# Scanning steps' orders made anew, and stage A's transposed x stored in DRAM and loaded by stage C in place of a second transpose

## What is computed

```
xr, gate = split(x @ W_in.T);  xr += cond
xc = silu(causal_conv4(xr) + b_conv)
xn = layernorm(xc) * g + b
B, C, dt = split(xn @ W_xproj.T);  dt = tanh(dt @ W_dt.T + b_dt) * 0.01
h_t = clip(h_{t-1} * (1 + dt_t * A) + B_t * min(|xn_t|, 1) * xn_t, -10, 10)   # 16 x 512 state per sequence
x1 = x + ((C_t . h_t) + D * xn) * silu(gate) @ W_out.T
z = layernorm(x1 * s1);  q, k, v = demodulated projections of z
out = x1 + demod(softmax(q k / 4) v @ W_w.T) + demod(v @ W_u.T)                # 16 heads of 16
```

## Time and profile before

| | us |
|---|---|
| median of 3 runs (1808.18 to 1811.61) | 1810.15 |
| the profiled execution, its own time | 1813.53 |
| its span, first to last instruction | 1811.8 |
| TensorE busy (share of the span) | 1594.8 (88%) |
| VectorE busy | 1402.2 (77%) |
| GpSimd busy | 1196.3 (66%) |
| ScalarE busy | 1136.2 (63%) |
| DMA packets' share of 16 engines, all on one queue | 51.8% |
| moved by DMA | 226.37 MB |

### The profile page before, as it was taken

One profiled execution on the slowest core, in us unless ns is written; L12 is line 12 of the kernel. 1 busy time (PEld: TensorE's weight loads), 2 busy tenths in 40 slices (PEclk: granted clock), 3 DMA queues, 4 the chain that ended last, 5 costly groups with the idle time before them and its releaser, 6 DMA issues. The chain is left out here.

```text
span 1811.8 us, 41467 instructions
## 1 busy us (share of the span) xinstructions
PE 1594.8 (88%) x12460; PEld 1036.9 (57%) x12460; DVE 1402.2 (77%) x2354; ACT 1136.2 (63%) x2913; POOL 1196.3 (66%) x1849
## 2 busy tenths in 40 slices
PE   5438688999999999999999999999899999989886
PEld 5423245666656565656665665656566665546664
DVE  1758677888878888888888788888888888778542
ACT  5664455767667676767676666667676666333552
POOL 0576577787777778777877777777777778323231
PEclk8667789999999999999999999999999999999997
DMA  4135565465555556655665655665556656445220
GB/s 105 45 89 116 113 144 134 121 141 143 130 140 140 133 145 148 148 136 128 140 143 129 142 136 135 145 152 134 140 126 138 150 131 153 114 112 125 66 65 24
DMA packets 223116, 226.37 MB, mean 125 GB/s; under 512 B 53488, under 2 KB 179056, under 8 KB 222896
## 3 DMA queue, kind: packets, MB, share of 16 engines
q1 hardware_dynamic: 222896, 223.71, 51.8%
HBM read 152.45 MB, written 71.17 MB: 123 GB/s over the span
## 5 line engine op out<-in xcount | busy, mean ns | idle before, releaser
L1704 DVE CUSTOM_DVE_ANT_0 gc<-ps_u,gc,hi 128x512 f32<-128x512 f32 x1008 | 812.0, 806 | 75.0 <-issue 2.2
L985 PE MATMUL ps_y<-gc,cms 128*32 128x512 f32 x2048 | 286.4, 632 | 0.3 <-DVE gc L1704 0.2
L970 PE MATMUL ps_u<-xs_sb,stage 64*128 64x512 bf16 x1024 | 201.2, 435 | 69.8 <-issue 51.5
L1286 ACT ACTIVATE a_tap<-a_xr,conv_w 128x128 f32<-128x128 f32 x768 | 244.2, 398 | 8.6 <-DVE a_xr L1636 8.6
L1303 ACT ACTIVATE a_z<-ps,a_nb,a_rs 128x512 f32<-128x512 f32 x64 | 49.7, 777 | 183.1 <-POOL a_nb L583 183.1
L1051 PEld LDWEIGHTS ps<-c_zT,L1T 128*128 128x128 f32 x1024 | 121.2, 194 | 70.9 <-issue 70.6
L550 POOL TENSOR_TENSOR a_tap<-a_tap 128x512 f32<-128x512 f32 x116 | 147.7, 1275 | 16.1 <-ACT a_tap L1286 16.1
L970 PEld LDWEIGHTS ps_u<-xs_sb,stage 64*128 64x128 bf16 x1024 | 76.7, 186 | 137.0 <-issue 92.7
L1051 PE MATMUL ps<-c_zT,L1T 128*128 128x128 f32 x1024 | 130.7, 281 | 24.3 <-DVE c_o L1788 21.0
L923 PE MATMUL ps<-a_xT,WinT 128*128 128x128 f32 x1024 | 139.3, 294 | 10.4 <-ACT a_xT L1276 9.4
L923 PEld LDWEIGHTS ps<-a_xT,WinT 128*128 128x128 f32 x1024 | 133.2, 210 | 16.5 <-ACT a_xT L1276 10.1
(11 more groups left out here) (180 smaller groups left out, 3555.3 us busy)
## 6 DMA issues: line engine op xcount, KB each, us to landing
xs_sb<-xn_parts SPq DMA_DIRECT2D x256, 192.0 KB
xn_parts<-a_parts SPq DMA_DIRECT2D x128, 192.0 KB, 3.0
skip_d_xn<-a_dx SPq DMA_DIRECT2D x64, 256.0 KB, 2.2
xs_sb<-xn_parts SPq DMA_DIRECT2D x128, 128.0 KB
scan_out<-y_sb SPq DMA_DIRECT2D x256, 64.0 KB
c_dx<-skip_d_xn SPq DMA_DIRECT2D x64, 256.0 KB, 6.0
c_y<-scan_out SPq DMA_DIRECT2D x64, 256.0 KB, 5.5
c_wu<-style_rows SPq DMA_DIRECT2D x128, 128.0 KB, 4.3
```

The lines of the kernel that those rows point to most:

```text
L970: pe.matmul(ps_u[r][t % 2][:, :], weights[:, :, l * SPAN + 2 * t + r], xs_sb[rows, sig % 2, t, :], start=True, stop=True).then_inc(s[f"b_u ...
L985: pe.matmul(ps_y[quad:quad + 32, :], cms[:, sig % 2, v, r, 32 * u:32 * (u + 1)], gc[r][:, (2 * u + v) % RING, :], start=(u == 0), stop=(u ...
L1286: ins = act.activation(a_tap[:, tap, m, :].rearrange("p (r t) -> p r t", r=2), a_xr[:, m, :, tap:tap + S], ACT.Identity, bias=bias, scale= ...
L1704: dve._custom_dve(bass.dve_ops.TENSOR_ADD_SAT, out=gc[r][:, t % RING, :], in0=ps_u[r][t % 2][:, :], in1=before, s0=hi[:, c % 4, col:col + ...
```

## The change

Stage A's `a_xT` is also stored to a DRAM tensor (`store_xT`), and stage C loads it (`load_xT`) into `c_xT` 13 steps later. `c_transpose_x` and `c_take_xT` are gone. SP issues both new DMAs between `load_cx` and `store_b`, and `load_w` is moved behind `load_dx` and `load_y`. ScalarE's `a_take_xT` also waits for the last tile's store. The lists of all phases but `first_step` are in a new order on TensorE, ScalarE, VectorE and GpSimd, with new PSUM banks. The core of the diff, with the full phase's lists whole (in the order GpSimd full, late and last; TensorE full and last; ScalarE full; VectorE full):

```diff
+        xT_dram = nc.dram_tensor("x_transposed", [TILES, P, KC * TOK], F32).ap()
...
+            def store_xT(n):
+                if not on(n):
+                    return
+                sp.wait_ge(s["a_xT"], at(n))
+                sp.dma_start(xT_dram[n], a_xT[:, :, :].rearrange("p k t -> p (k t)")).then_inc(s["a_st_xT"], 16)
+
+            def load_xT(n):
+                if not on(n):
+                    return
+                sp.wait_ge(s["a_st_xT"], at(n, 16))
+                sp.wait_ge(s["c_gate"], at(n - 1))
+                sp.dma_start(c_xT[:, :, :].rearrange("p k t -> p (k t)"), xT_dram[n]).then_inc(s["c_ld_xT"], 16)
+
             def load_cx(n):
                 if not on(n):
                     return
-                sp.wait_ge(s["c_xTp"], at(n - 3))
                 sp.wait_ge(s["c_x1"], at(n - 3))
...
                 store_y(sig - 1)
                 load_x(i + 1)
                 load_cx(c0 + 1)
+                store_xT(i)
+                load_xT(c0 + 1)
                 if chain_due(i, 1) is not None:
                     store_b(chain_due(i, 1))
-                    load_w(chain_due(i, 1))
                 load_dx(c0 + 1)
                 load_y(c0 + 1)
+                if chain_due(i, 1) is not None:
+                    load_w(chain_due(i, 1))
                 load_wu(c0 - 2)
...
-            def c_transpose_x(n, b):
-                if not on(n):
-                    return
-                pe.wait_ge(s[f"c_ld_x{n % 3}"], at(n // 3, 16))
-                ps = take(b, (s["c_xT"], at(n)))
-                for k in range(KC):
-                    mm = pe.transpose(ps[:, k * TOK:(k + 1) * TOK], c_x[:, n % 3, k * P:(k + 1) * P], ident[:, :])
-                mm.then_inc(s["c_xTp"], 1)
-
             def c_project_gate(n, b):
                 if not on(n):
                     return
-                pe.wait_ge(s["c_xT"], at(n))
+                pe.wait_ge(s["c_ld_xT"], at(n, 16))
                 ps = take(b, (s["c_sg"], at(n)))
...
+                act.wait_ge(s["a_st_xT"], at(n - 1, 16))
...
             def step(i):
                 sig, c0 = i - SCAN_LAG, i - C_LAG
                 spread_c(sig)
-                a_second_rest(i - 3)
-                c_bias(c0 - 1)
                 a_var(i - 2)
                 a_root(i - 2)
                 a_bias(i - 2)
                 if chain_due(i, 1) is not None:
                     split_b(chain_due(i, 1))
+                a_half(i - 1, 0)
+                a_second_rest(i - 3)
+                a_offset(i - 2)
+                a_gain(i - 2)
                 c_sum_skip(c0)
                 c_gate_product(c0)
-                a_gain(i - 2)
+                c_bias(c0 - 1)
                 a_shift(i - 2)
                 a_scale_b(i - 3)
-                a_offset(i - 2)
-                a_half(i - 1, 0)
-                a_skip(i - 2)
                 a_half(i - 1, 1)
                 a_sum(i - 1)
                 c_join(c0 - 3)
+                c_style(c0)
+                a_first_rest(i - 2)
                 a_norm_root(i - 2)
-                c_style(c0)
+                a_skip(i - 2)
+                c_final(c0 - 3)
                 c_var(c0)
-                c_final(c0 - 3)
-                a_first_rest(i - 2)
                 c_root(c0)
 
             def late_step(i):
                 sig, c0 = i - SCAN_LAG, i - C_LAG
                 spread_c(sig)
-                c_bias(c0 - 1)
                 if chain_due(i, 1) is not None:
                     split_b(chain_due(i, 1))
                 c_sum_skip(c0)
                 c_gate_product(c0)
+                c_bias(c0 - 1)
                 c_join(c0 - 3)
                 c_style(c0)
                 c_final(c0 - 3)
@@ -820,14 +837,14 @@
 
             def last_step(i):
                 c0 = i - C_LAG
+                c_sum_skip(c0)
                 c_bias(c0 - 1)
-                c_sum_skip(c0)
                 c_gate_product(c0)
+                c_style(c0)
                 c_join(c0 - 3)
-                c_style(c0)
                 c_var(c0)
+                c_final(c0 - 3)
                 c_root(c0)
-                c_final(c0 - 3)
 
             for i in range(STEP_COUNT):
...
             def step(i):
                 sig, c0 = i - SCAN_LAG, i - C_LAG
-                a_project_bc(i - 3, 2)
-                c_transpose_x(c0, 0)
-                c_transpose_z(c0 - 2, 1)
+                c_weigh_v(c0 - 3, 0)
+                a_project_bc(i - 3, 1)
+                c_transpose_z(c0 - 2, 2)
                 scan_block(sig, 0)
-                a_transpose_x(i, 2)
-                c_project_gate(c0, 0)
-                a_transpose_xc(i - 2, 1)
-                c_weigh_v(c0 - 3, 2)
-                scan_block(sig, 1)
-                c_project_qv(c0 - 2, 2)
                 c_transpose_o(c0 - 3, 0)
                 c_project_k(c0 - 2, 1)
+                a_transpose_xc(i - 2, 2)
                 c_project_wu(c0 - 3, 0)
+                c_project_qv(c0 - 2, 1)
+                scan_block(sig, 1)
+                a_transpose_x(i, 1)
+                c_scores(c0 - 2, 0, 2)
+                c_project_gate(c0, 1)
+                a_project_in(i, 0)
                 scan_block(sig, 2)
-                c_transpose_yg(c0, 1)
-                a_project_in(i, 0)
-                c_scores(c0 - 2, 2, 1)
-                c_transpose_v(c0 - 2, 0)
+                c_transpose_yg(c0, 0)
+                c_transpose_p(c0 - 2, 1, 1)
+                c_transpose_v(c0 - 2, 2)
+                c_transpose_p(c0 - 2, 0, 0)
+                c_project_out(c0, 1)
+                a_transpose_bc(i - 3, 0)
                 scan_block(sig, 3)
-                a_transpose_bc(i - 3, 0)
-                c_project_out(c0, 2)
-                c_transpose_p(c0 - 2, 0, 1)
-                c_transpose_p(c0 - 2, 1, 0)
...
             def last_step(i):
                 c0 = i - C_LAG
-                c_transpose_x(c0, 0)
-                c_transpose_z(c0 - 2, 2)
+                c_project_gate(c0, 2)
+                c_transpose_z(c0 - 2, 0)
                 c_weigh_v(c0 - 3, 1)
-                c_project_k(c0 - 2, 2)
-                c_project_gate(c0, 0)
-                c_transpose_o(c0 - 3, 1)
-                c_project_qv(c0 - 2, 2)
-                c_project_wu(c0 - 3, 1)
-                c_scores(c0 - 2, 0, 2)
-                c_transpose_yg(c0, 1)
+                c_project_qv(c0 - 2, 0)
+                c_transpose_o(c0 - 3, 2)
+                c_project_k(c0 - 2, 1)
+                c_project_wu(c0 - 3, 2)
+                c_scores(c0 - 2, 1, 2)
+                c_transpose_yg(c0, 0)
+                c_project_out(c0, 0)
+                c_transpose_p(c0 - 2, 1, 2)
                 c_transpose_v(c0 - 2, 1)
-                c_project_out(c0, 0)
-                c_transpose_p(c0 - 2, 0, 2)
...
             def step(i):
                 sig, c0 = i - SCAN_LAG, i - C_LAG
-                c_take_xT(c0, bank[0])
+                c_take_zT(c0 - 2, bank[2])
+                a_take_tap(i - 1, 3)
+                c_take_oT(c0 - 3, bank[0])
+                b_take_y(sig - 1)
+                c_block_keys(c0 - 2, bank[1])
                 a_take_tap(i - 1, 1)
+                a_take_tap(i - 1, 0)
+                a_second_part(i - 3)
+                a_normalise(i - 2, bank[2])
+                c_double_v(c0 - 2)
+                a_take_xT(i, bank[1])
+                c_tanh(c0, bank[1])
+                c_exp(c0 - 2, 1)
+                c_exp(c0 - 2, 0)
+                c_take_ygT(c0, bank[0])
+                c_take_pT(c0 - 2, 1, bank[1])
+                a_square_sum(i - 2)
+                c_take_pT(c0 - 2, 0, bank[0])
+                c_block_values(c0 - 2, bank[2])
+                a_take_bcT(i - 3, bank[0])
+                a_first_part(i - 2)
+                c_normalise(c0 - 1)
+                a_take_tap(i, 2)
+                a_tanh(i - 1)
...
             def step(i):
                 sig, c0 = i - SCAN_LAG, i - C_LAG
+                c_invert(c0 - 3, bank[0])
                 c_stats(c0 - 1)
+                a_take_bc(i - 3, bank[1])
+                c_divide(c0 - 3, bank[0])
+                scan_step(sig, 0, 0)
+                a_silu(i - 2)
                 c_mean_var(c0 - 1)
-                a_take_bc(i - 3, bank[2])
-                scan_step(sig, 0, 0)
                 scan_step(sig, 0, 1)
-                a_silu(i - 2)
+                if chain_due(i, 1) is not None:
+                    prepare(chain_due(i, 1))
+                a_stats(i - 2, bank[2])
+                a_mean_var(i - 2)
                 scan_step(sig, 1, 0)
                 scan_step(sig, 1, 1)
-                c_silu(c0, bank[0])
-                a_stats(i - 2, bank[1])
-                a_mean_var(i - 2)
-                c_invert(c0 - 3, bank[2])
-                c_divide(c0 - 3, bank[2])
+                c_demodulate(c0 - 3, bank[0])
+                c_scale_q(c0 - 2, bank[1])
+                c_scale_v(c0 - 2, bank[1])
```

(35 more changed lines are left out.)

192 lines of the change are left out of this document (80 added, 112 removed).

## The result

The changed kernel took 1846.32 us (median; 1838.87 to 1848.19) against 1810.88 of the kernel before on the same chip: a ratio of 1.018, interval 1.015 to 1.022. It is slower by 33 us between the two profiled executions and by 35 between the medians, where 1799 had been forecast. The profiled execution took 1846.59, against the 1802 that the sum made on that basis.

What follows compares the result with a forecast made beforehand. TensorE was taken to bound ordinary steps, SP's serial queue the change of chain. Terms -1 (rounds), -2.5 (other full steps), -5.5 (last chain), -2.5 (last phase) and 0 sum to -11.5: from 1810.15 to 1799 us, range 1769 to 1824.

Steps and rivals of the forecast that it cites:

- Ordinary steps: Full-phase steps without a change of chain: 23.93 us falls to 23.4, 0.53 less, from two waits and a transpose gone.
- near meeting: Two possible new TensorE waits, at `a_transpose_xc` and `a_project_in`: together between 0 and 0.99 us a step, 0.46 taken.
- wait ahead of `c_project_gate`: TensorE's possible wait for the new load: taken as nothing; any such wait would show the forecast wrong.
- The change of chain: Preparing step, counted from its `scan_block 0` (B): later `a_skip` and `load_raw` bring the weights 2.0 us later; round 99.6 us.
- rival 2: Change of chain: weights 2.5 us a round later still, through added DMAs and a later `a_skip`; 1829 us, chance 0.20.
- The 3.95 us: Time a round of the kernel before takes beyond four ordinary steps (99.67 - 4 x 23.93), assigned to the change of chain.
- The later weights cover it: Preparing step: VectorE's stop for raw data costs up to 2 us, hidden by the later weights, so nothing added.
- The two new DMAs: `store_xT` and `load_xT` in SP's queue ahead of `store_b`: about 0.45 us each to issue.
- The last chain: `store_out` and all behind it about 6.5 us sooner, less 0.45 for an added load: -5.5 us, bounds 0 and -7.2.
- last phase: Steps of 14.90 us lose a transpose and two waits but gain new ones: -0.6 a step, -2.5 for four.
- Stages A and B alone: Phase where `prepare` and `split_b` come first, but `store_b` goes by SP's queue: 0 us, bounds -3 and +3.
- Rival 1: Weights stay where they were and no new wait appears: round 96.7 us, 1764 us in all, chance 0.15.

Runs made afterwards that it cites:

- e7: Changed kernel with GpSimd's `a_skip` directly ahead of `c_style`: 1803.1 us, ratio 0.992 to the kernel before.
- e4: Changed kernel with `store_xT` and `load_xT` moved behind `load_w`: 1834.9 us, ratio 1.012 to the kernel before.
- e3: Changed kernel with `load_raw` ahead of `store_dx` in SP's list, nothing else: 1823.0 us, ratio 1.004 to the kernel before.
- e9: Changed kernel with VectorE's `prepare` back behind the third sub-step's scan: 1833.5 us, ratio 1.014 to the kernel before.
- e5: Changed kernel, SP reordered: `load_raw` before `store_dx`, `store_b` between `load_xs` and `store_y`, `load_w` behind `load_cx`, then `store_xT`, `load_xT`: 1758.4 us, ratio 0.968 to kernel before.
- e10: Changed kernel with the SP order of e5 and the `a_skip` move of e7 together: 1734.9 us, ratio 0.959 to the kernel before.
- e1: Kernel before with second transpose and its eviction replaced by `store_xT` and `load_xT` ahead of `store_b`, old orders otherwise: 1839.4 us, ratio 1.014.
- e8: Kernel before with only x's detour through DRAM, its `store_xT` and `load_xT` behind `load_w`: 1812.8 us, ratio 0.998.
- e11: As e10, with VectorE's `prepare` back behind the third sub-step's scan: 1783.1 us, ratio 0.986 to the kernel before.
- e12: Kernel before with `load_raw` ahead of `store_dx`, `store_b` between `load_xs` and `store_y`, `load_w` behind `load_cx`: 1793.3 us, ratio 0.991.
- e6: Kernel before with `store_b` moved between `load_xs` and `store_y` and `load_w` behind `load_cx`: 1800.5 us, ratio 0.992.

## Why the prediction was wrong

*Ordinary steps: right.* Forecast 23.4, measured 23.47. The waits for `c_o` and for the bank of `a_add_style` went. One near meeting, `a_transpose_xc`, costs 0.23 us (it starts 1.12 us after the group ahead of it in an ordinary step, 850.70 to 851.82, and 0.90 after it in e7); `a_project_in` costs nothing in the kernel after, and 0.5 us a round for `c_s` once the raw data are early. No wait ahead of `c_project_gate`.

*The change of chain: the step that failed.* "So `a_skip` ends about B + 0.5, and `load_raw` starts at B + 1.0": measured B + 1.75 and B + 2.20. I had followed `a_skip`'s partners on ScalarE and missed that of `c_style`, which the new order puts ahead of `a_first_rest`. It waits 1.53 us for ScalarE's `c_z`. ScalarE's first part, for which I had let `a_first_rest` wait, is ready at 790.64 (its instruction starts at 790.01 and takes 0.63); `a_first_rest` starts at 791.99, 1.35 us later, behind `c_style`. That is the 1.25 us by which `a_skip` was missed. That e7 moves `a_skip` ahead of `c_style` and gets 43 us (2.6% by ratios) shows what a late `a_skip` costs as a whole, the part that I had foreseen included. Behind the late raw data the whole chain slid: `store_b` B + 16.89 (forecast 14.7), first product B + 30.76 (forecast 28.70, before 26.70). Of the 2.2 us by which `store_b` missed, 1.2 are `load_raw`'s, 0.66 `load_xT`'s wait for the gate product, which I had taken as ready, and 0.3 a shorter gain between `load_raw` and `load_xs` than the 1.1 us that I counted on. From `store_b` on the forecast's durations held: 5.25 to `load_w`, 4.41 from the issue's end to the product. In the mean of twelve chains the first product comes at B + 30.5 where it came at 27.2 before, and from it to the next B it is 71.8 us instead of 72.5: the ordinary steps' gain, less the slow stretches. Together that is the measured 102.26. It is 2.7 us beyond the forecast, just past rival 2's price (2.5); rival 2's mechanism, later weights through the added DMAs and a later `a_skip`, was the true one, though it too has no term for the clock. Twelve rounds of it make 32 of the 45 us by which the profiled execution missed 1802.

The 3.95 us that the prediction gave to the change of chain were not all the wait for the weights: 1.1 us of them were the wait for `c_yg` in the preparing step, which the new order took away, and a slow stretch stood behind the weights' wait in 8 of 12 rounds.

*"The later weights cover it": wrong in its consequence.* The stop of VectorE was foreseen, at up to 2 us, and set to nothing. It took 2.45 us in the chain shown and stopped TensorE for 2.08 us, let the clock fall, and made the gate product later, behind which `load_xT` and `store_b` stood: `load_xT` was issued 0.66 us after SP was free, and with it out of the way (e4) 11 us came back. The cover itself was real in good part: e3, rid of the stop, got 2.8 us back in the preparing step and lost 1.6 of them to a longer wait for the weights. A clean price no run gives: e3 also brought the weights 1.7 us nearer to B, and e9 took the stop away and got another for it.

*The clock* had no term. The 9169 instructions of twelve rounds are busy for 1165 us in the kernel after and 1124 to 1130 in e5 and e10: 35 to 41 us. By the estimate from granted clocks 32 to 38 of these are the clock (39 us of work lost against 2 in e5 and 7 in e10).

*The two new DMAs:* 0.9 us for the issues was right for what SP does, and too little for what it delays (e1: 1.3 us a chain in the first product's wait, 24 us in all; e8: nothing once they stand behind `load_w`).

*The last chain and last phase:* the queue did what was forecast. No `a_skip` stood ahead of `load_raw`, `store_out` followed it at once, and from `load_raw` to the first product it was 27.62 us (1610.63 to 1638.25) instead of 34.58, 7.0 less where 6.05 was forecast. TensorE, which before had stood 2.64 us for `c_o` in that step, reached the wait sooner as well, so its idle time fell by 2.7 us only. The forecast's -5.5 was a gain of time written down against that idle time. Steps -0.23 us where -0.6 was taken, for the two new waits. Both directions right.

*Stages A and B alone:* set to 0 (bounds 3), measured +6.9. Not taken apart; but in e3, which moves `load_raw` ahead of `store_dx` and nothing else, the first product of that chain comes at 300.50 instead of 312.18 (302.00 in e5), so it is again `load_raw`'s place behind the late `store_dx`.

*Rival 1* (1764: orders' gain kept, weights in place) is what e5 and e10 show to be possible, and more; it was wrong for SP's and GpSimd's orders as the change had them.

## What to carry over

Where a queue issues in order, ask for each move on another engine which DMA stands behind the moved instruction's store: here one operation, moved behind three others on GpSimd, held `load_raw` by 3.5 us and turned 0.8% gained into 1.8% lost. For an operation that is moved, follow the waits of every operation it now stands behind, not only its own. And price a stop on TensorE with the slow stretch that may follow it: here 2.08 us idle were followed by 4 us that did the work of 2.3, so the two were of a size.

## What the chip showed beside it

- Stops of 1.6 and 0.5 us were followed by 4 us at a granted clock of 0.57; over twelve rounds the same products took 3% longer than in e5. A slow stretch lasted 3 to 3.5 us in most cases, and 5.5 to 7 in many behind the longer waits of e1 and e3. Not every stop had one: in e11, with one stop of 3.4 to 3.7 us a round, 10 of 12 were followed by it; behind the one that ended at 691.46 the granted clock was 0.52 for the next 3 us, behind that at 789.88 it was 1.00. In the kernel before it were 8 of 12.
- From the issue of `store_b` to the `load_w` that waits for its landing: 5.25 us in the kernel after and 5.39 in that before in the chains shown, where single loads stand just ahead of it, but 7.62 in e5 and 7.95 in e10 (752.70 to 760.65), where it is issued directly behind the six DMAs of `load_xs`. In the mean of twelve chains it is 5.6 and 6.1 (up to 6.5 in the other kernels with that place), against 7.8 and 7.6. What was just ahead makes the difference here, not what comes behind: e12 and e6 have `store_b` in the same place of the list, with the same `store_y` behind it, but issue it 3.5 us after `load_xs` has ended, as the parts are late, and take 5.5 and 6.1. Of the 6.9 us that the earlier place gained in e5 (B + 9.5 against B + 16.5) 2.2 went back that way.
- 7.4% more bytes (243.14 MB against 226.37) did not make the two landings on the weights' way later (e8).
